# Token layers of a language-model tower: projected rows fetched by indirect DMAs instead of encodings times weights on TensorE

## What is computed

```python
enc = one_hot(token_ids, 512) + sinusoidal_pe            # [8, 256, 512]
def layer(enc, (wq, wk)):                                # 4 layers, wq and wk are [512, 128]
    q, k = enc @ wq, enc @ wk
    sims = where(causal, q @ k.T / sqrt(128), -1e9)
    return softmax(sims) @ enc
```

## Time and profile before

| | |
|---|---|
| median of 3 runs | 2302.99 us (2301.66 to 2303.2) |
| span of the profiled execution, first to last instruction | 2301.2 us |
| median over that span | 1.8 us |
| PE busy | 2220.2 us, 96% of the span |
| DVE, ACT, POOL busy | 1656.8, 715.0, 381.6 us |
| start of the next stage's matmuls (L794) | 255.4 us |

### The profile page before, as it was taken

The page is one execution under the profiler, slowest core; times in us unless marked ns, Lnnn a source line. Parts: engine busy times, 40 slices in busy tenths (PEclk is TensorE's granted clock), DMA queues, the critical chain, the costliest instruction groups (busy, mean ns, idle before and its releaser), DMA issues.

```text
span 2301.2 us, 31084 instructions
## 1 busy us (share of the span) xinstructions
PE 2220.2 (96%) x11962; PEld 1130.5 (49%) x11962; DVE 1656.8 (72%) x3357; ACT 715.0 (31%) x1603; POOL 381.6 (17%) x416
## 2 busy tenths in 40 slices
PE   6777899999999999999999999999999999999999
PEld 4666444444444444444445555555555554444444
DVE  7767799998998886576766665665665677588832
ACT  5667423122122112444333333333333333211111
POOL 3453100000000330622050002100400300401000
PEclk9889999999999999999999999999999999999999
DMA  6767733333323333221231112311311223100001
GB/s 188 223 185 215 244 131 106 108 133 119 126 98 119 124 126 117 60 81 53 71 94 35 35 29 53 90 29 35 101 35 35 63 65 62 60 1 1 1 1 74
DMA packets 195683, 202.73 MB, mean 88 GB/s; under 512 B 148944, under 2 KB 161872, under 8 KB 186576
## 3 DMA queue, kind: packets, MB, share of 16 engines
q1 hardware_dynamic: 195248, 199.70, 29.0%
q10 hardware_dynamic: 288, 1.05, 0.1%
HBM read 137.28 MB, written 27.26 MB: 72 GB/s over the span
## 4 chain that ended last, share of the span: by engine, by line
PE 86%; DVE 6%; issue 3%; ACT 2%; POOL 1%; DMA 1%; SPq 0%; DVEq 0%; POOLq 0%
PE ps L794 22%; PE ps L250 14%; PE ps L1415 9%; PE ps L806 7%; PE ps L1218 7%; PE ps L1231 6%; PE ps L687 5%; PE ps L1047 4%; PE ps L1064 4%; PE ps L1256 2%; PE ps L264 2%; PE ps L500 1%; PE ps L1259 1%; PE ps L262 1%; PE ps L641 1%
## 5 line engine op out<-in xcount | busy, mean ns | idle before, releaser
L794 PE MATMUL ps<-planes 128*128 128x512 f16 x1224 | 269.7, 379 | 0.0
L794 PE MATMUL ps<-planes,wa 128*128 128x512 f16 x1080 | 237.8, 379 | 2.1 <-DVE planes L1521 2.1
L250 PE MATMUL ps<-planes,wa 128*128 128x512 f16 x840 | 192.3, 379 | 3.2 <-DVE planes L1774 3.2
L794 PEld LDWEIGHTS ps<-planes 128*128 128x128 f16 x1224 | 119.8, 98 | 141.5
L834 ACT ACTIVATE work<-work 128x512 f16<-128x512 f32 x64 | 40.3, 630 | 440.1 <-DVE work L867 440.1
L250 PE MATMUL ps<-planes 128*128 128x512 f16 x768 | 175.9, 379 | 0.9 <-DVE planes L667 0.9
L794 PEld LDWEIGHTS ps<-planes,wa 128*128 128x128 f16 x1080 | 105.6, 98 | 127.5 <-issue 2.6
L311 ACT ACTIVATE ps<-ps,nmax 128x128 f32<-128x128 f32 x160 | 54.4, 340 | 307.5 <-DVE nmax L305 307.5
L621 POOL TENSOR_TENSOR rstd<-rstd,half 128x4 f32<-128x4 f32 x16 | 17.9, 1117 | 754.3 <-DVE rstd L616 754.2
L949 DVE COPY_PREDICATED work<-work 128x1024 f32<-128x1024 int16 x144 | 119.6, 830 | 21.3 <-DVE work L931 0.5
L931 DVE TENSOR_SCALAR work<-work,lutx,par 128x256 int32<-128x256 int32 x384 | 128.1, 408 | 0.0
(11 more groups left out here) (199 smaller groups left out, 4242.9 us busy)
## 6 DMA issues: line engine op xcount, KB each, us to landing
planes<-rw SPq DMA_DIRECT2D x17, 2048.0 KB, 8.5
wa<-rw SPq DMA_DIRECT2D x15, 2048.0 KB, 7.3
stg<-in_rw_w SPq DMA_DIRECT2D x32, 512.0 KB, 4.9
stg<-in_ff_w SPq DMA_DIRECT2D x16, 1024.0 KB, 5.6
rw<-wa SPq DMA_DIRECT2D x16, 1024.0 KB, 7.7
stg<-in_mo_w SPq DMA_DIRECT2D x16, 1024.0 KB, 5.6
work<-in_glu_idx SPq DMA_DIRECT2D x48, 128.0 KB, 2.1
glu_dec<-work SPq DMA_DIRECT2D x48, 128.0 KB, 1.7
```

The costliest lines, as they stand in the source:

```text
L250: mm = te.matmul(ps[:, bank, :], w(i, kt), x(j, kt), start=(kt == 0 and n == 0), stop=(kt == KT - 1 and n == 2))
L794: mm = te.matmul(ps[:, what, :], rw_w(q, what, i, kt, m), mix[what][j][:, kt, at:at + CH], start=(kt == 0 and z == 0), stop=(kt == KT - 1 ...
```

## The change

The products of encodings and weights are no longer computed for every token. At the start SP copies the 512 rows of Wq_l and Wk_l into two tables in DRAM: `tab_first` for layer 0 (a row is 256 floats, 1 KB) and `tab_rest` for layers 1 to 3 (768 floats, 3 KB), in 8 DMAs DRAM to DRAM. PE makes the position part pe · [Wq_l, Wk_l] once for all four layers (`tok_pew`: 32 float32 matmuls of 256 columns). For each chunk ACT copies the position part to where the rows go (`first_act`, one copy of 128x1024; `more_act`, six copies of 128x512), and POOL fetches the token rows on top of it with indirect DMAs that add: four of 128 rows for layer 0 (`gather_first`; chunk 0 is fetched plainly and DVE adds the position part, `first_dve`) and four for layers 1 to 3 (`gather_more`). Layer 0's q and k are then eight float32 transposes a chunk instead of 24 matmuls. Layers 1 to 3 split the fetched rows with one ACT copy and one DVE subtraction of 128x1024 per (layer, chunk), both from SBUF (`ew_act`, `ew_dve`), placed by EW_AT.

What goes: `tok_ew` with L1641 and L1755, `cols_dve`, `cols_act`, `cols_lo`, the split of the token weights (L1655, L2096), the load of the broadcast ids (1 MB), and SP's waits ahead of the first `load_rw32` and `load_abs`. The wait of `load_rw(0)` becomes one for the last unit's projection. `setup()` moves to the front of DVE's program, and its wait is for the last of SP's 15 first DMAs. The encodings by rows for `tok_out` stay. The bodies of `first_act` and `gather_first` are like those of `more_act` and `gather_more`, with the wait `first_sum` for chunks 2 and 3.

```diff
+        tab_first = nc.dram_tensor("tab_first", (D, 2 * P), F32, kind="Internal").ap()
+        tab_rest = nc.dram_tensor("tab_rest", (D, (LAYERS - 1) * 2 * P), F32, kind="Internal").ap()
...
-        def tok_project0(pe, u, c, q, bank, done):
-            if q == 0:
-                pe.wait_ge(enc_lo, KT * (c + 1))
-                pe.wait_ge(w_ready, 1)
-            pe_project(u, bank, done, lambda i, kt: TOK_W[:, i, 0, q, kt, :], lambda j, kt: tokT[j][:, kt, c * CH:c * CH + CH])
+        def tok_project0(pe, c):
+            if c == 0:
+                pe.wait_ge(first_sum, 1)
+                pe.wait_ge(ident_in, 16)
+            else:
+                pe.wait_ge(first_in[c], 64)
+            for q, done in ((0, q_ps), (1, k_ps)):
+                for j in range(TPC):
+                    mm = te.transpose(ps[:, q, j * P:j * P + P], first_tile(c, j)[:, q * P:q * P + P], ident[:, :])
+                mm.then_inc(done, 1)
...
-        def tok_ew(pe, u, b):
...
+        def tok_pew(pe, l):
+            if l == 0:
+                pe.wait_ge(pet_in, 16)
+            pe.wait_ge(tw_in[l], 16)
+            for x in range(2):
                 for kt in range(KT):
-                    for n, (i, j) in enumerate(PASSES):
-                        mm = te.matmul(ps[:, ew_bank(u, b), z * S:z * S + S].rearrange("p (q d) -> p q d", q=2),
-                                       tokT[j][:, kt, tt * P:tt * P + P], TOK_W[:, i, l + 1, :, kt, :],
-                                       start=(kt == 0 and n == 0), stop=(kt == KT - 1 and n == 2))
-            mm.then_inc(ew_ps, 1)
+                    mm = te.matmul(ps[:, PEW_BANK[l], x * S:x * S + S].rearrange("p (q d) -> p q d", q=2), peT[:, kt, x * P:x * P + P],
+                                   TOK_W[:, l, :, kt, :], start=(kt == 0), stop=(kt == KT - 1))
+            mm.then_inc(pew_ps, 1)
...
-        COLS_AT = {0: (8, 9), 1: (10, 11), 2: (12, 13), 3: (14, 15)}
+        EW_AT = {2: [(1, 1)], 3: [(2, 1), (3, 1)], 5: [(1, 2)], 6: [(2, 2), (3, 2)], 8: [(1, 3)], 9: [(2, 3), (3, 3)]}
+        MORE_AT = {1: 1, 4: 2, 7: 3}
...
         def tok_pe(pe):
...
+            tok_pew(pe, 0)
+            for l in range(1, LAYERS):
+                tok_pew(pe, l)
+            tok_project0(pe, 0)
+            tok_scores(pe, 0)
...
-                if l < LAYERS - 1:
-                    tok_ew(pe, u, 0)
...
-                if l < LAYERS - 1:
-                    tok_ew(pe, u, 1)
...
+        def more_act(act, c):
+            if c == 0:
+                act.wait_ge(pew_sb, LAYERS - 1)
+            else:
+                act.wait_ge(ew_lo, ew_nth(LAYERS - 1, c - 1))
+            for l in range(1, LAYERS):
+                for b in range(2):
+                    dst = more_rows.rearrange("p (t l d) -> p t l d", t=TPC, l=LAYERS - 1)[:, 2 * b:2 * b + 2, l - 1, :]
+                    ins = se.activation(dst, pew_part(l).rearrange("p (t d) -> p t d", t=2), ACT.Copy)
+            ins.then_inc(rest_pre, 1)
...
+        def ew_act(act, which):
+            for l, c in which:
+                act.wait_ge(more_in[c], 64)
+                if l == LAYERS - 1:
+                    act.wait_ge(pew_ps, LAYERS)
+                se.activation(ew_chunk(l, 0, c), more_chunk(l), ACT.Copy).then_inc(ew_hi, 1)
...
         def tok_act(act):
-            tok_w_act(act, 0)
-            cols_act(act, (0, 1))
-            tok_w_act(act, 1)
-            cols_act(act, (2, 3, 4, 5))
+            first_act(act, 1)
+            for l in range(1, LAYERS):
+                pew_act(act, l)
             act_q(act, 0)
             act_k(act, 0)
-            cols_act(act, (6, 7))
+            more_act(act, 0)
             act_exp(act, 0)
...
+            first_act(act, 2)
             act_q(act, 1)
             act_k(act, 1)
...
+            first_act(act, 3)
+            ew_act(act, [(1, 0)])
             act_exp(act, 1)
+            ew_act(act, [(2, 0), (3, 0)])
             rw_split_act(act, 0)
...
                 rw_split_act(act, u)
-                if l < LAYERS - 1:
-                    tok_act_ew(act, u, 1)
+                ew_act(act, EW_AT.get(u, ()))
...
+                if u in MORE_AT:
+                    more_act(act, MORE_AT[u])
...
+        def ew_dve(dve, which):
+            for l, c in which:
+                dve.wait_ge(ew_hi, ew_nth(l, c))
+                ve.tensor_tensor(ew_chunk(l, 1, c), more_chunk(l), ew_chunk(l, 0, c), ALU.subtract).then_inc(ew_lo, 1)
...
         def tok_dve(dve, chain, setup):
...
+            setup()
+            first_dve(dve)
...
+            store_rows(0, 0), store_rows(0, 1)
+            sp.dma_start(tok_rows_i, a["tok_rows"]).then_inc(ids_in, 16)
+            sp.dma_start(peT.rearrange("p k t -> p (k t)"), a["consts"][:, K_PET:K_PET + KT * S]).then_inc(pet_in, 16)
+            sp.dma_start(ident[:, :], a["consts"][:, 0:P]).then_inc(ident_in, 16)
+            for l in range(1, LAYERS):
+                store_rows(l, 0), store_rows(l, 1)
...
-            sp.wait_ge(w_ready, LAYERS - 1)
             load_rw32(0, 0), load_rw32(0, 1)
+            load_abs(0)
             sp_p1(sp, 0)
-            sp.wait_ge(w_ready, LAYERS)
-            load_abs(0)
...
-                        sp.wait_ge(ew_ps, 2 * (MU - NC))
+                        sp.wait_ge(k_ps, MU)
...
+            def gather_more(c):
+                pool.wait_ge(rest_pre, c + 1)
+                for j in range(TPC):
+                    at = bass.IndirectOffsetOnAxis(ap=tok_rows_i[:, c * TPC + j:c * TPC + j + 1], axis=0)
+                    ge.indirect_dma_start(out=more_tile(j), out_offset=None, in_=tab_rest, in_offset=at,
+                                          compute_op=ALU.add).then_inc(more_in[c], 16)
+            pool.wait_ge(ids_in, 16)
+            pool.wait_ge(tab_in[0], 32)
+            gather_first(0)
+            pool.wait_ge(first_pre, 1)
+            gather_first(1)
+            pool.wait_ge(tab_in[1], 32 * (LAYERS - 1))
+            gather_more(0)
+            for c in range(2, NC):
+                pool.wait_ge(first_pre, c)
+                gather_first(c)
             for u in range(MU):
...
                 rw_split_pool(pool, u)
+                if u in MORE_AT:
+                    gather_more(MORE_AT[u])
```

More of the change, by code:

```diff
@@ L1577, in tok_pe @@
         def tok_pe(pe):
-            pe.wait_ge(w_ready, 1)
-            for kt in range(KT):
-                pe.wait_ge(enc_lo, kt + 1)
-                for q, done in ((0, q_ps), (1, k_ps)):
-                    for n, (i, j) in enumerate(PASSES):
-                        mm = te.matmul(ps[:, q, :], TOK_W[:, i, 0, q, kt, :], tokT[j][:, kt, 0:CH], start=(kt == 0 and n == 0),
-                                       stop=(kt == KT - 1 and n == 2))
-                    if kt == KT - 1:
-                        mm.then_inc(done, 1)
-            tok_scores(pe, 0, 0)
-            tok_ew(pe, 0, 0)
+            tok_pew(pe, 0)
[3 more added lines that the diff above has]
+            tok_scores(pe, 0)
             tok_project(pe, 1)
             pe.wait_ge(probs, 1)
-            tok_ew(pe, 0, 1)
-            tok_scores(pe, 1, 0)
+            tok_scores(pe, 1)
+            pe.wait_ge(first_pre, NC - 1)
+            pe.wait_ge(pew_sb, LAYERS - 1)
             for u in range(1, MU - 2):
@@ L2161, in _ @@
         def _(act):
-            se.dma_start(stg[:, 0, 0:1024], a["tok_w"][0]).then_inc(stg_full[0], 16)
-            se.dma_start(stg[:, 1, 0:1024], a["tok_w"][1]).then_inc(stg_full[1], 16)
+            for l in range(LAYERS):
+                se.dma_start(tok_w32[:, l * 1024:l * 1024 + 1024], a["tok_w"][l]).then_inc(tw_in[l], 16)
             tok_act(act)
```

224 lines of the change are left out of this document (85 added, 139 removed).

## The result

The changed kernel takes **2345.9 us** (median of 4 runs, 2340.59 to 2351.37) against 2302.6: a ratio of 1.0184 [1.0168, 1.0201]. The forecast was 2293, the range ended at 2320: wrong in sign and in size. The profiled execution spans 2344.8 us. The stage behind the token layers (L821, before: L794) begins at 299.09 us in place of 255.38, and lasts 2344.8 - 299.1 = 2045.7 us as before (2045.8): all 43.7 us are lost in the token stage.

What follows compares the result with a forecast made beforehand. The token stage, the first 257 us, was taken as bound by a chain of waits between engines, with DMA queues close behind. -30 + 11 + 3 + 2 + 4 = -10 us gave 2293 us; range 2270 to 2320.

Steps and rivals of the forecast that it cites:

- ACT's wait for the fetches: In the loop, ACT waits for fetches placed only one unit ahead: 4 us for the last three chunks.
- The landing: Time for a chunk's fetched 1.6 MB to arrive: 6 us, between 4 and 11, from 1 MB in 7.0 us.
- the DMA share: Busy share of the DMA engines in the token stage, 0.69 before: expected at 0.75 to 0.85 after the change.
- POOL's issues: POOL's time to issue an indirect fetch: 1.2 us each, between 0.4 and 2.7, counted in the start's delay.
- What goes there really shortens a unit: From 110 to 257 us, removing the encodings-times-weights matmuls and their splits takes 30 us off the chain.
- copies and splits: In the loop after 110 us: one `more_act` on the chain costs 3 us, the splits of fetched rows 2 us.
- The start: Position parts, copies, issues and landing make unit 2's scores 11 us later, including first scores 8 us later.
- Rival 3: Fetches hold POOL and, behind it, ACT, once a chunk's issue and landing exceed about 18 us: 2319 us, chance 0.20.
- Rival 2: DMA gives the gain back through 9.4 MB more of fetches and tables: 2303 us, chance 0.15.
- Rival 4: PE has less work and its clock falls, so transposes and scores double in seven units: 2306 us, chance 0.09.
- Rival 1: The whole chain share comes out, 53 us, as DMA doesn't hold the early stretch: 2275 us, chance 0.20.
- the 150 that would have spoken for rival 3: Sign in the token stage: POOL busy for over 150 us would show the forecast wrong.

Runs made afterwards that it cites:

- e7_nofetch: The changed kernel without the fetches of the token rows for layers 1 to 3, everything else kept; 2304.1 us, ratio 1.0006 to the kernel before.
- e12_narrow: e6_both with fetches for layers 1 to 3 of 512 bytes a row in place of 3072, as many issues; 2322.8 us, ratio 1.0088 to the kernel before.
- e6_both: The changed kernel with SP's transposes waiting for the fetches of chunks 0, 2 and 3, and chunks 2 and 3 fetched one unit earlier; 2330.6 us.
- e8_clock: e6_both with 24 float16 matmuls, whose result nobody reads, added behind the scores of units 2 to 9; 2328.7 us, ratio 1.0114 to the kernel before.
- m1_micro: A separate kernel timing fetches, DMA transposes and loads alone and in pairs; four plain fetches took 8.6 us, beside transposes 17.6.

## Why the prediction was wrong, step by step

- **ACT's wait for the fetches: 4 us booked for the last three chunks, about 46 measured** (5.7, 16.5 and 23.5 us, where under 2 each were forecast). This step failed first. All that the fetches of layers 1 to 3 cost is 42 us by e7_nofetch. The landing was sized from a 1 MB load (6 us, at most 11); from the start of the last issue it took 10.4, 10.1, 15.8 and 23.3 us. Bytes and the DMA share were looked at; which kinds of transfer meet was not. Placing the fetch only one unit ahead left no room for it.
- **POOL's issues: no price behind the start.** 1.85 us with its gap was within the bounds (1.2, 0.4 to 2.7). Twelve behind the start are 22 us of POOL. By e12_narrow at most 19 us of the time go with the issues, though POOL idles for half of the stage. The forecast called its idle time cover; what the traces show in its place is a burst of POOL's work behind the issues, and long DVE operations beside it.
- **"What goes there really shortens a unit", -30 us: it didn't.** Measured without fetches: 8 us from unit 2 to 15, and 5.5 us from unit 6 on, where the 30 were booked and 5 for copies and splits taken off. Two thirds of the matmuls put back cost 2 us by the medians, 6.3 by the start of the next stage. The operands standing ready at 174.74 us showed PE on the chain in that unit, not that DVE, POOL and the loads would have let the next one begin sooner. So the forecast would have missed without the fetches too: e7_nofetch takes 2304.1 us.
- **The start: 11 us booked, 16 came** (unit 2 at 61.66 against 45.50). First scores were at 29.76 us (28 forecast), the 32 matmuls at 15.8 us (16.7): right. The rest is the issue, 1.85 us each (1.2), and the landing, 8.9 us behind the last issue's end (6). Without the fetch 5.6 us of it remain. It doesn't end at unit 2: POOL's first weight split starts at 57.3 us (39.59 before), and in e7_nofetch, with 50.7, unit 3's scores come at 71.0 us in place of 60.1.
- **Rival 3 named the side and the way**, fetches that hold ACT and POOL, and its point of decision, issue and landing over 18 us, was passed by chunks 2 and 3 with 3 x 1.85 + 15.8 = 21.4 and 3 x 1.85 + 23.3 = 28.8 us. Its price, 2319, fell short because 11 us bounded the landing. **Rival 2** (bytes): 8 us, between e6_both and e12_narrow. **Rival 4**: the clock fell, to 0.75 in the stage; e8_clock, which gives part of it back, is no faster, and the price of the rest wasn't measured. **Rival 1** fell with the -30. The page "DMA: Bandwidth & Descriptors" of the Trainium skill ("Anatomy of one DMA — SWDGE (gpsimd) path") gives, as an estimate by its fit, 2.9 us for a fetch; alone in m1_micro, a plain one landed 3.5 us after the end of its issue, beside transposes 12.5.
- **Held:** nothing moved behind the stage; the DMA share is 0.82 in it (0.75 to 0.85); POOL, busy for 149.6 us of it, stayed just under the 150 that would have spoken for rival 3.

Open: why DVE gets no turn in POOL's burst; how the 19 us between e12_narrow and e7_nofetch divide between DVE's rows, POOL's lateness, SP's wait and the placement; by what way fetches and transposes slow each other in the kernel; and why the clock falls near 1168 us of e7_nofetch, behind pauses of PE (0.39, 0.67 and 1.18 us) like those of before.

## What to carry to other kernels

In a ring of engines a line's share of the chain is the most that its removal can give, and the second bound decides how much comes: put work of the same size in that nobody reads, or look for what is ready a few us behind. Price a new transfer by the kinds that it will meet, DMA transposes above all, and place it ahead by that landing. Count POOL's issues as work of POOL, 1.85 us each here: what piles up behind them runs as one burst, and beside it DVE operations with two SBUF inputs took up to 8.25 us. Before pricing a wait in the trace, look whether an edit that removes it moves something else as well, as the earlier placement did.

## What the runs showed of the hardware

- An indirect fetch of 128 rows occupies POOL for 0.95 us (plain, 3072 B a row) or 1.54 us (adding, the same for 512 and 3072 B a row) and 0.30 us to the next.
- Four plain fetches of 393 KB beside four DMA transposes of 128x768 float16 take 17.6 us, more than one after the other (15.4); four adding ones take 16.8, less than the sum (20.2). In the kernel, with loads and a store beside them, the queues were busy at 21 to 37 GB/s for 8.7 us.
- Six DVE operations with both inputs in SBUF take 9.4 us beside POOL's in place of 3.7, with one input in PSUM 3.7 in both; an adding fetch's issue grows from 1.56 to 2.08 us beside the first kind.
- Between 60 and 110 us PE's granted clock was 0.57 in e6_both and 0.74 in e8_clock, where matmuls had been added, at the same time of the kernel. Far behind the token stage it fell once more in e7_nofetch: 0.91 from 1160 to 1200 us, where the kernel before has 1.00.
